# Query and key projections of the wide heads from seven block products a pair of heads

## The reference, cut to what matters

```
def _cross_attention(q_in, kv_in, wq, bq, wk, bk, wv, bv, wo, bo, bias_k, bias_v):
    b, q_len, _ = q_in.shape
    t = kv_in.shape[1]
    qh = (q_in @ wq + bq).reshape(b, q_len, H, K)
    kh = (kv_in @ wk + bk).reshape(b, t, H, K)
    vh = (kv_in @ wv + bv).reshape(b, t, H, K)
    kh = jnp.concatenate([kh, jnp.broadcast_to(bias_k, (b, 1, H, K))], axis=1)
    vh = jnp.concatenate([vh, jnp.broadcast_to(bias_v, (b, 1, H, K))], axis=1)
    scale = jnp.sqrt(jnp.asarray(K, q_in.dtype))
    logits = jnp.einsum('bqhk,bthk->bhqt', qh, kh) / scale
    weights = jax.nn.softmax(logits, axis=-1)
    ctx = jnp.einsum('bhqt,bthk->bqhk', weights, vh).reshape(b, q_len, H * K)
    return ctx @ wo + bo
```

## Time and profile before

| | us |
|---|---|
| median of 3 runs | 1532.59 (1530.67 to 1536.9) |
| profiled execution, its own time | 1532.62 |
| its span | 1530.8 |
| PE busy | 1467.0 (96%) |
| PEld busy | 1131.2 (74%) |
| DVE busy | 914.4 (60%) |
| ACT busy | 900.7 (59%) |
| POOL busy | 140.9 (9%) |

### The profile page before, as it was taken

One profiled execution on the slowest core, in us unless ns is written; L12 is line 12 of the kernel. 1 busy time (PEld: TensorE's weight loads), 2 busy tenths in 40 slices (PEclk: granted clock), 3 DMA queues, 4 the chain that ended last, 5 costly groups with the idle time before them and its releaser, 6 DMA issues.

```text
span 1530.8 us, 28652 instructions
## 1 busy us (share of the span) xinstructions
PE 1467.0 (96%) x9824; PEld 1131.2 (74%) x9824; DVE 914.4 (60%) x3306; ACT 900.7 (59%) x2807; POOL 140.9 (9%) x171
## 2 busy tenths in 40 slices
PE   7999999999999999999999999999899998999996
PEld 5766688878787877787878787878666666866664
DVE  4777832445454555554545454531899996158997
ACT  5878934444344344444444343433899997379996
POOL 2010011000000000100000000011222322012200
PEclk9999999999999999999999999999999999999999
DMA  7000003001010100101001000000100100000000
GB/s 297 2 2 1 31 35 124 1 28 36 1 63 1 48 15 1 63 1 49 15 1 64 1 1 0 1 0 1 56 1 9 36 15 8 1 1 9 15 2 22
DMA packets 10879, 40.66 MB, mean 27 GB/s; under 512 B 2416, under 2 KB 2672, under 8 KB 8688
## 3 DMA queue, kind: packets, MB, share of 16 engines
q1 hardware_dynamic: 10736, 38.82, 7.0%
HBM read 37.77 MB, written 1.05 MB: 25 GB/s over the span
## 4 chain that ended last, share of the span: by engine, by line
PE 66%; ACT 17%; DVE 4%; issue 3%; DVEq 0%; POOLq 0%; ACTq 0%; POOL 0%
ACT probs L1000 11%; PE bank L829 7%; PE bank L810 7%; PE bank L843 7%; PE bank L802 7%; PE bank L789 7%; PE bank L792 7%; PE bank L769 5%; PE bank L758 5%; ACT pT L1008 5%; PE bank L818 4%; PE bank L603 2%; PE bank L587 1%; DVE probs L1265 1%; DVE probs L1247 1%
## 5 line engine op out<-in xcount | busy, mean ns | idle before, releaser
L1000 ACT ACTIVATE probs<-probs,negmax 128x256 f32<-128x256 f32 (+1 forms) x640 | 349.4, 559 | 41.7 <-DVE negmax L1265 41.1
L1081 ACT ACTIVATE pT<-bank 128x512 f32<-128x512 f32 x128 | 76.4, 597 | 388.0 <-PE bank L818 388.0
L603 PEld LDWEIGHTS bank<-ident,probs 128*128 128x128 f32 x1536 | 167.6, 141 | 119.4 <-ACT probs L1000 60.3
L603 PE MATMUL bank<-ident,probs 128*128 128x128 f32 x1536 | 226.1, 280 | 28.8 <-ACT pT L1008 17.5
L1410 DVE TENSOR_REDUCE stats<-bank 128x1 f32<-128x257 f32 x256 | 108.5, 425 | 212.2 <-PE bank L810 211.2
L1265 DVE CUSTOM_DVE_ANT_0 probs<-bank,mask_a 128x256 f32<-128x256 f32 (+1 forms) x384 | 173.8, 508 | 28.6 <-PE bank L587 23.8
L1008 ACT ACTIVATE pT<-bank 128x512 f32<-128x512 f32 x288 | 170.9, 595 | 6.9 <-PE bank L603 6.7
L829 PE MATMUL bank<-pT,probs 128*128 128x256 f32 x512 | 132.7, 381 | 2.7 <-ACT pT L1081 2.7
L810 PE MATMUL bank<-kT,pT 128*128 128x257 f32 x512 | 132.7, 382 | 0.6 <-ACT pT L1064 0.6
L1000 ACT ACTIVATION_READ_ACCUMULATOR probs<-probs,negmax 128x1 f32 x640 | 132.7, 207 | 0.0
L1072 ACT ACTIVATE probs<-bank,stats 128x257 f32<-128x257 f32 x256 | 118.4, 473 | 3.5 <-DVE stats L1413 3.5
(11 more groups left out here) (111 smaller groups left out, 2472.0 us busy)
## 6 DMA issues: line engine op xcount, KB each, us to landing
w_m<-in_w SPq DMA_DIRECT2D x6, 1024.0 KB, 6.9
g_qkv<-in_g SPq DMA_DIRECT2D x4, 1536.0 KB, 7.0
q_res<-in_g SPq DMA_DIRECT2D x4, 1536.0 KB, 6.3
w_qkv<-in_w SPq DMA_DIRECT2D x3, 768.0 KB, 4.3
g_bv<-in_gbv SPq DMA_DIRECT2D x8, 256.0 KB, 7.0
g_o<-in_go SPq DMA_DIRECT2D x4, 512.0 KB, 3.4
q_res<-in_go SPq DMA_DIRECT2D x4, 512.0 KB, 3.5
rows<-in_rows SPq DMA_DIRECT2D x1, 1664.0 KB, 14.0
```

Source lines behind the costliest of these rows:

```text
L603: last = nc.tensor.transpose(out[:, n * P:(n + 1) * P], probs[:, u % PROBS, q * T + t * P:q * T + (t + 1) * P], ident[:, :])
L1000: last = nc.scalar.activation(s, s, ACT.Exp, bias=negmax[:, u % PROBS, k:k + 1], scale=-1.0, accum_out=sums[:, tile % 2, q, j * c.res + r: ...
```

## The change

A wide layer now works on pairs of heads m (32 a layer). For one pair and one batch, q is a product of a 256 x 256 block of weights (2 heads by 2 blocks of features) with 256 x 256 of x (2 blocks of features by 2 of rows); the same for k with ctx. As 128 x 128 blocks that is eight products each. They are now formed from seven each, with sums of blocks in front (GpSimd: `row_sums` of ctx and of the normed x, `weight_sums` a group and pair) and behind. Writing the head first and the rows second, the first chain (`add_r1`, bank 2, four steps) accumulates, and after each of its steps ScalarE reads the bank as it stands into one block of q and k (`read_r1`). The second chain (`add_r2`, bank 5, three steps) is added to three of these blocks by VectorE. q and k of a step stand side by side in a bank, 128 columns each. The bank of the second chain was one of the two of y; y is now in one bank, added by one instruction of 512 columns.

The first two pairs of a layer (DIRECT = 4 heads) go by the former kq, two of these heads ahead of the loop where one was. A pair m is worked on in the two iterations n = 2m-4 and n = 2m-3: in the even one the last step of the pair before in the second chain, steps 0 and 1 of the first and step 0 of the second; in the odd one steps 2 and 3 of the first, step 1 of the second. Each iteration has two points for them: behind the transposes, and in front of project.

The extra sums lie in mask_a, mask_m, v_four, kT, pT and probs, whose other uses move: the clearing of v_four and the loads of mask_2 and the first mask_2c go behind the second wide layer's products.

```diff
-KQ_BANK, T_BANK, PV_BANK, V_BANK, Y_BANK = 2, 4, 6, 7, [3, 5]
+KQ_BANK, SUM_BANK, Y_BANK, T_BANK, PV_BANK, V_BANK = 2, 5, 3, 4, 6, 7
...
+PAIRS = HEADS // 2
+DIRECT = 4
...
+        def pair(m):
+
+            return m // (2 * B), m // 2 % B, m % 2, m - DIRECT // 2
+
+        def heads_at(m, h, t):
+
+            return qk1[:, (2 * m + h) % 4, 0:2 * T].rearrange("p (w t) -> p w t", w=2)[:, :, t * P:(t + 1) * P]
...
+                def blocks(m, w):
+
+                    g, b, x, _ = pair(m)
+                    at = [slice((2 * x + h) * P, (2 * x + h + 1) * P) for h in range(2)]
+                    src = ctxT if w else hT
+                    return (lambda h, k: g_qkv[g % 2][:, w, k, at[h]], lambda s: w_sum[:, x, s - 1, w, :],
+                            lambda k, t: src[:, b, k, t * P:(t + 1) * P],
+                            lambda s: (c_sum if w else h_sum)[b][:, s - 1, :])
+
+                def add_r1(m, step):
+
+                    g, b, x, i = pair(m)
+                    pe.wait_ge(sem("b_r1out"), st.at("b_r1out", 0, 4 * i + step))
+                    if step == 0 and i == 0:
+                        pe.wait_ge(sem("b_kq"), st.at("b_kq", 0, DIRECT))
+                    if step == 0 and b == 0 and x == 0:
+                        weights("c_qkv", g, 16)
+                    if step == 0 and g == 0 and x == 0:
+                        rows_turned(pe, before, b)
+                    if step == 1:
+                        pe.wait_ge(sem("b_wsum"), st.at("b_wsum", 0, 2 * g + x + 1))
+                        pe.wait_ge(sem("b_hsum"), st.at("b_hsum", 0, B if g else b + 1))
+                        if i == 0:
+                            pe.wait_ge(sem("b_csum"), B)
+                    for w in range(2):
+                        wt, ws, xt, xs = blocks(m, w)
+                        one, two = [(wt(0, 0), xt(0, 0)), (ws(2), xs(2)), (ws(3), xs(3)), (wt(1, 1), xs(4))][step]
+                        last = mm(bank[KQ_BANK][:, w * P:(w + 1) * P], one, two, start=(step == 0 and w == 0),
+                                  stop=(step == 3), skip_group_check=True)
+                    last.then_inc(sem("b_r1"), 1)
+
+                def add_r2(m, step):
+
+                    g, b, x, i = pair(m)
+                    pe.wait_ge(sem("b_r2out"), st.at("b_r2out", 0, 3 * i + step))
+                    if step == 0 and i == 0:
+                        pe.wait_ge(sem("b_kq"), st.at("b_kq", 0, DIRECT))
+                    for w in range(2):
+                        wt, ws, xt, xs = blocks(m, w)
+                        one, two = [(wt(0, 1), xt(1, 0)), (ws(1), xs(1)), (ws(4), xt(1, 1))][step]
+                        last = mm(bank[SUM_BANK][:, w * P:(w + 1) * P], one, two, start=(step < 2 and w == 0),
+                                  stop=(step != 1), skip_group_check=True)
+                    last.then_inc(sem("b_r2"), 1)
...
                 def scores(n):
-                    pe.wait_ge(sem("b_kq"), st.at("b_kq", 0, n + 1))
+                    if n < DIRECT:
+                        pe.wait_ge(sem("b_kq"), st.at("b_kq", 0, n + 1))
+                    else:
+                        i = pair(n // 2)[3]
+                        pe.wait_ge(sem("b_r1out"), st.at("b_r1out", 0, 4 * (i + 1)))
+                        pe.wait_ge(sem("b_r2out"), st.at("b_r2out", 0, 3 * (i + 1)))
                     pe.wait_ge(sem("b_exp"), st.at("b_exp", 0, n))
                     for q in range(QT):
-                        mm(bank[q][:, 0:K1], qT1[:, n % 2, q * P:(q + 1) * P], kT1[:, n % 2, :],
+                        mm(bank[q][:, 0:K1], qk1[:, n % 4, q * P:(q + 1) * P], qk1[:, n % 4, T:T + K1],
                            start=True, stop=True).then_inc(sem("b_scores"), 1)
...
-                        last = mm(bank[Y_BANK[q]][:, 0:D], oT1[:, n % H1, q * P:(q + 1) * P], g_o[g % 2][:, h, :],
-                                  start=(h == 0), stop=(h == H1 - 1 and not with_key))
+                        last = mm(bank[Y_BANK][:, q * D:(q + 1) * D], oT1[:, n % H1, q * P:(q + 1) * P], g_o[g % 2][:, h, :],
+                                  start=(h == 0 and q == 0), stop=(h == H1 - 1 and not with_key), skip_group_check=True)
...
+                kq(2)
+                kq(3)
                 for n in range(HEADS):
+                    m = n // 2 + DIRECT // 2
...
-                    if n + 2 < HEADS:
-                        kq(n + 2)
+                    if n % 2 == 0:
+                        if n and m <= PAIRS:
+                            add_r2(m - 1, 2)
+                        if m < PAIRS:
+                            add_r1(m, 0)
+                    elif m < PAIRS:
+                        add_r1(m, 2)
+                        add_r2(m, 1)
...
+                    if m < PAIRS:
+                        if n % 2 == 0:
+                            add_r1(m, 1)
+                            add_r2(m, 0)
+                        else:
+                            add_r1(m, 3)
                     if n >= 1:
                         project(n - 1)
...
+                def read_r1(m, step):
+
+                    g, b, x, i = pair(m)
+                    act.wait_ge(sem("b_r1"), st.at("b_r1", 0, 4 * i + step + 1))
+                    h, t = [(0, 0), (0, 1), (1, 1), (1, 0)][step]
+                    to, at = heads_at(m, h, t), g * H1 + 2 * x + h
+                    if step == 0:
+
+                        act.wait_ge(sem("b_scores"), st.at("b_scores", 0, 2 * (2 * m - 2)))
+                        for y in range(2):
+                            nc.scalar.activation(qk1[:, (2 * m + y) % 4, 2 * T:T + K1], col(f"key{j}", at + y), ACT.Copy)
+                    for w in range(2):
+                        last = nc.scalar.activation(to[:, w, :], bank[KQ_BANK][:, w * P:(w + 1) * P], ACT.Identity,
+                                                    bias=col(("bq", "bk")[w] + str(j), at))
+                    last.then_inc(sem("b_r1out"), 1)
...
-                kq(1)
+                for n in range(1, DIRECT):
+                    kq(n)
...
-                    if n + 2 < HEADS:
-                        kq(n + 2)
+                    if m < PAIRS:
+                        read_r1(m, 2 * (n % 2))
                     if h == 0 and u > UNITS - B:
                         learned_weights(u - (UNITS - B) - 1)
+                    if m < PAIRS:
+                        read_r1(m, 2 * (n % 2) + 1)
...
-                    for q in range(QT):
-                        xq = x_rows[:, b * QT + q, :]
-                        last = v.tensor_tensor(xq, bank[Y_BANK[q]][:, 0:D], xq, ALU.add)
-                    last.then_inc(sem("b_yout"), 1)
+                    xb = x_rows[:, both(b), :]
+                    v.tensor_tensor(xb, bank[Y_BANK][:, :].rearrange("p (q d) -> p q d", q=QT), xb, ALU.add)\
+                        .then_inc(sem("b_yout"), 1)
...
+                def add_r2(m, step):
+
+                    i = pair(m)[3]
+                    dve.wait_ge(sem("b_r1out"), st.at("b_r1out", 0, 4 * i + (1, 3, 2)[step]))
+                    dve.wait_ge(sem("b_r2"), st.at("b_r2", 0, 3 * i + step + 1))
+                    to = heads_at(m, *[(0, 0), (1, 1), (0, 1)][step])
+                    v.tensor_tensor(to, bank[SUM_BANK][:, 0:2 * P].rearrange("p (w t) -> p w t", w=2), to, ALU.add)\
+                        .then_inc(sem("b_r2out"), 1)
...
+                    if n and n % 2 == 0 and m <= PAIRS:
+                        add_r2(m - 1, 2)
...
+                    if m < PAIRS:
+                        add_r2(m, n % 2)
...
+            def row_sums(to, src, b, name):
+
+                b11, b12, b21, b22 = [src[:, b, k, t * P:(t + 1) * P] for k in range(KT) for t in range(2)]
+                n = next(steps)
+                nc.gpsimd.tensor_tensor(to[:, 0, :], b12, b11, minus).then_inc(sem("p_one"), 1)
+                nc.gpsimd.tensor_tensor(to[:, 2, :], b22, b12, minus)
+                pool.wait_ge(sem("p_one"), n)
+                nc.gpsimd.tensor_tensor(to[:, 1, :], b22, to[:, 0, :], minus).then_inc(sem("p_two"), 1)
+                pool.wait_ge(sem("p_two"), n)
+                nc.gpsimd.tensor_tensor(to[:, 3, :], b21, to[:, 1, :], minus).then_inc(sem(name), 1)
...
+                to = w_sum[:, x, :, :, :]
+                n = next(steps)
+                nc.gpsimd.tensor_tensor(to[:, 0, :, :], a21, a22, add).then_inc(sem("p_one"), 1)
+                nc.gpsimd.tensor_tensor(to[:, 2, :, :], a11, a21, minus)
+                pool.wait_ge(sem("p_one"), n)
+                nc.gpsimd.tensor_tensor(to[:, 1, :, :], to[:, 0, :, :], a11, minus).then_inc(sem("p_two"), 1)
+                pool.wait_ge(sem("p_two"), n)
+                nc.gpsimd.tensor_tensor(to[:, 3, :, :], a12, to[:, 1, :, :], minus).then_inc(sem("b_wsum"), 1)
...
+            pool.wait_ge(sem("s_rest"), 32)
+            pool.wait_ge(sem("a_pv"), end("a0", "a_pv"))
             for b in range(B):
+                row_sums(c_sum[b], ctxT, b, "b_csum")
+            weight_sums(1, 0, 0)
```

(56 more changed lines are left out.)

41 lines of the change are left out of this document (29 added, 12 removed).

## The result

The changed kernel takes 1560.2 us, the median of 4 runs (1559.9 to 1561.8), where before took 1531.9 beside it: a ratio of 1.0181, 95% interval 1.0169 to 1.0192. The forecast was 1554. The profiled execution has a span of 1558.1 us, 27.3 more than before, where the sum of the prediction had 21.1.

The account below looks back on a forecast made before the run. TensorE, busy 377.57 of 381 us in layer 1 of the wide attention, bounds the kernel. Span 1530.8 + 18.9 (two layers) + 2.2 (GpSimd at the start) = 1551.9, so 1554 us; range 1534 to 1580.

Parts of the forecast that it names:

- The product count: TensorE's q and k: 28 records of 0.111 us a pair, 3.11 us for 3.46, 21.0 us saved over two layers.
- Rival 3: TensorE's weight loads not covered at 128 columns; at 0.14 us a record, 1584 us; chance 0.10.
- the estimate of 0.156: TensorE's time in us per 128-column record, taken from the skill page as a ratio; sum some 1600 us.
- ScalarE's free time and the read: ScalarE free 2.90 us after the scores' start; a read's two 128x128 activations take 0.26 + 0.37 us.
- Rival 2: ScalarE's reads as short as 128x1 activations (0.09 spacing, 0.19): 18 us less a layer, 1536 us, no change; chance 0.12.
- The iterations: TensorE in wide layers: h = 0 5.60 us, h = 3 4.98, h = 1 6.14, h = 2 6.58; a unit 0.82 longer.
- The count of waits: TensorE's long waits on ScalarE's 128x128 activations: 26 a layer, 0.5 to 0.8 us, in h = 0 and h = 3.
- it costs nothing, but has little cover left: VectorE's add behind the maxima in h = 2 pushes the values add to end just ahead of TensorE's 3.12 us.
- GpSimd at the start: GpSimd's 24 sums ahead of l11's first power, 12.0 us, delay the rows TensorE wants at 218.36: +2.2 us.
- Busy PE down by tens of us while the span grows: Sign expected in the profile: TensorE's busy time falls by tens of us although the whole run gets longer.
- Rival 1: ScalarE's reads are in time and only the product count is felt in TensorE: 1514 us; chance 0.10.
- Iteration 60: Near a wide layer's end, TensorE's iteration loses its kq: 3.99 us in all, was 4.98.

Follow-up runs that it names:

- e10: Changed kernel, project mostly ahead of times_v, values' add first, weight sums and key copies later, add of y ahead of maxima in h = 1: 1517.8 us, ratio 0.9900.
- e1: Changed kernel with TensorE's second point behind project instead of in front of it: 1530.8 us, ratio 0.9987 to the kernel before.
- e5: Changed kernel with ScalarE reading an iteration's first step ahead of the exponentials instead of behind them: 1535.0 us, ratio 1.0018 to the kernel before.
- e2: Changed kernel with VectorE's values add ahead of the third add of the second chain in h = 2: 1557.6 us, ratio 1.0163 to the kernel before.
- e3: Changed kernel with GpSimd's sums of the first group's weights behind the first power and bias of l11: 1556.0 us, ratio 1.0154 to the kernel before.

## Why the prediction was right

The sign, the place and the mechanism were right, and the size was short by 6 us of 28.

- **The product count.** 0.111 us a record was forecast, 0.112 measured. Rival 3 is out, and with it the estimate of 0.156 from the Trainium skill ("TensorE: Matmul & The Clock Gate", Back-to-back issue gap): in this f32 stream the pairs of load and product at 128 columns come at 0.112. The saving of 0.70 us a unit is seen almost whole in e10 (0.67).
- **ScalarE's free time and the read.** Forecast 2.90 and 0.63 for two activations, measured 2.90 and 0.63. One takes 371 ns on the mean of 480, forecast 0.37. The 387 ns worked out from the Trainium skill ("ScalarE: Activation LUTs", What ACT_TABLE_LOAD costs) were 4% high. Rival 2 is out.
- **The iterations.** h = 3 forecast 4.98, measured 4.99; h = 0 5.60 and 5.63; h = 2 6.58, and 6.68 or 6.74 measured. e1 and e5 take the same wait away from two engines' sides, and either gives back 25 to 29 us. The count of waits was exact.
- **The step that failed: "it costs nothing, but has little cover left".** VectorE's add came when it was forecast, but I compared its end with the start of the values product. In `values` the wait for the bank stands in front of the weight load as well as of the product, and that load runs under times_v; so the bank must be free before. (Whether the load alone could go ahead of it, no run tested.) h = 2 is 0.10 us over the forecast in 24 places and 0.16 in six, 3.4 us; e2 gives 2.6 of it back.
- **The term that was too small: GpSimd at the start.** Forecast +2.2 us; by e3 it is 4.1. The sums of 128x128 took 0.41 to 0.54 us start to start where I took 0.4, and the wait was 2.98. The rest is in the main the clock, of which the sum had nothing.
- **"Busy PE down by tens of us while the span grows" was wrong.** In the two layers PE is busy 752.7 us of 777, and 759.9 of 767 before. Part of each wait is counted as busy: the wait in h = 0 costs 0.80 us (463.89 + 0.10 against 462.32 + 0.87), of which 0.46 is shown as idle, since the modelled ends of the products ahead of it run into it.
- **Rival 1** gave 1514 for a kernel without these waits. e10, which has none but those at the ends of the layers (2.4, 2.2, 2.0 and 1.5 us in its list of waits), takes 1517.8. Per unit its saving is whole, but from the first scores to the last of the two layers it is only 15.2 us shorter than before (730.0 for 745.2), not 20: the rest goes at the layers' ends, where two kq more stand in front (7.76 us between the first two scores for 4.31) and do not all come back.
- **Iteration 60.** The prediction gave it 4.98 us before and 3.99 after; measured 6.13 (991.85 to 997.98) and 5.15 (1021.82 to 1026.97). The product with the learned key's output that stands behind project there (L850 before, L929 after) was left out on both sides, so the difference, which is what the sum uses, comes out right.

In the spans the three parts are these. The two layers, from the first scores to the last, take 768.8 us for 745.2, 23.7 more, where the sum had 18.9; h = 2 has 3.4 of the 4.8 that are missing, the rest are hundredths in the other iterations. The first scores come 4.6 us later (262.21 for 257.65), where the sum had 2.2. The rest of the kernel is 1.0 us shorter, which no run here explains: that is luck, and without it the forecast would be 1 us further off. 21.1 + 4.8 + 2.4 - 1.0 = 27.3.

## What to carry to other kernels

On an engine that is full, a cut in its work is worth its size only if every result that it needs is still early: before counting the saving, go through the new order and set each wait's release time, worked out on the releasing engine in its own queue order, against the time at which the full engine now asks, which the cut itself moves ahead. A chain that accumulates in one bank and is read between its steps needs a piece of other work as long as the reader's queue behind each step; a single operation moved (project, 0.87 us) decided here between 1.8% slower and no slower. Where the wait for a bank stands in front of a product's weight load, as here, the time that counts is that of the load.

## What the runs showed of the hardware that was not expected

- After 2.98 us without work at a granted clock of 1.00, TensorE's clock was at its lower level for about 3.4 us, which cost 1.7 us; without that wait (e3) it stayed at 1.00. It is not certain to fall: in e2 it stayed at 1.00 after 3.02 us without work.
- Four records of 128 columns with full weights take 0.445 to 0.45 us, as four of 64 columns did: between 128 and 64 columns nothing is gained, and the number of loads and records, not of columns, sets the pace.
- A wait of a weight load hides in the pieces beside it: the matmuls' own list has no idle time for it. In the h = 2 of the changed kernel shown first times_v takes 0.99 us (450.59 to 451.58) and the values 1.79 (to 453.37). With the add ahead (e2) they take 0.92 and 1.72:

```profile
449.12 1.09 PE L908 MATMUL bank<-pT,probs 128*128 128x256 f32 x4
450.04 1.88 PE L876 MATMUL bank<-g_qkv,ctxT 128*128 128x512 f32 x4
451.76 0.38 PE L853 MATMUL bank<-mask_a,kT 128*128 128x128 f32 x2
```

The two differences of 0.07 are the 0.15 that e2 gave back in this iteration. In the 24 other places times_v takes its 0.92 and the values 1.80 (428.06 to 429.86): the whole 0.08 to 0.09 is in the values.
